# Half-wide one-hots by source-tile parity, and the input rows' inverse root made on GpSimd, in a graph network with a two-expert layer

## The chip, the cores and the metric

The kernel runs on one NeuronCore of a Trainium2 chip. Its engines work side by side, each from its own queue: TensorE (PE) multiplies, VectorE (DVE) and ScalarE (ACT) work elementwise, GpSimd (POOL) does a little, SyncE (SP) issues most DMAs. They hand work to each other through semaphores. The metric is the device time of one execution in microseconds (us); lower is better.

## The reference, cut to what matters

```python
deg  = segment_sum(ones, rows, N) + 1.0          # N = 6250 nodes, 100000 edges (rows, cols)
dinv = rsqrt(deg)[:, None]
h = layernorm(x) @ W_in + b_in                   # 256 features
for l in range(4):
    h_scaled = h * dinv
    msg = segment_sum(h_scaled[cols], rows, N) * dinv
    ctx = mean(h, axis=0) @ Wg[l] + bg[l]
    z = relu((h + msg) @ Wl[l] + bl[l] + ctx)
    h = layernorm(z) * gamma[l] + beta[l]
x = x + h
# then: x + layernorm(x + the two best of eight experts' feed-forward of layernorm(x))
```

`rows` is the input `src` and `cols` the input `dst`. The edges come sorted by `dst`.

## The kernel before

The kernel turns the edge list into a dense matrix of edge counts, the adjacency, of 49 by 49 tiles of 128 by 128 nodes in one byte each. It writes it to HBM and then, in each of the four layers, reads it back and multiplies the node table with it. The matrix is made in the first 512 us; the layers run until about 2830 us and the experts until the end.

The 100,000 edges lie in 782 blocks of 128, one per column, with an edge on each partition. For each destination tile `m` of 128 nodes the kernel takes a window of `WIN` = 18 neighbouring blocks. The destination one-hot `hot_d` says which of the tile's 128 nodes an edge goes to. The source one-hot `hot_s` is 540 wide: it has 11 columns (`LANES`) for each of the 49 source tiles, and twelve lanes share one column, told apart by the power of two in `src_w`, two bits each. The matmul of the two, summed over the window, gives for the tile's 128 nodes the counts of all sources, packed in words of 24 bits.

Four engines work on tile `m` or its neighbours at the same time:

- VectorE (`hots`, L713) makes the source one-hots, one per block (`tensor_scalar`, L724): 35 for each pair of tiles, since neighbouring windows overlap. Between them it makes the input rows' statistics (L731, L734), `mask` of the previous tile (L757, four shifts and masks over the words), `relative` (L700, the labels of the next window, whose start it loads into a register first, L699), the reciprocal and the bias of the row normalisation (L744, L747), and the label one-hots of the next tile (`hot_rows`, L708).
- TensorE (`counts`, L1269) multiplies, two matmuls of 270 columns for each block, and between them runs the transpose (`turn`, L1297) and the input product (`product`, L1302 and L1304) of the previous tile's normalised rows. Behind the counts come `degrees` of the previous tile (L1266, 49 matmuls of one column over the staged bytes) and `add_mean` (L1310).
- ScalarE (`extract`, L1102) takes the square root (L1105), copies the transpose out (xnT, L1108), runs `unpack` of the previous tile (L1094: twelve activations, each turning one two-bit field of the words into 11 lanes of bytes), normalises the next rows (xnb, L1112), copies the product (h0, L1100) and then the words of this tile (L1118).
- SyncE writes four tiles of staged bytes at a time to HBM (`write`, L493), from two halves of a buffer in turn.

The order on each engine is written out by hand and unrolled. `wait_ge` holds an engine until a semaphore has a value; nothing behind it on that engine starts earlier. The index of a one-hot's column, and the window's start, come from registers, which the engine's sequencer sets: these are the rows `ISA` and `TENSOR_LOAD` in the lists of order below.

Behind the last tile follow its degrees and product, a flag that says whether all edges were counted, the scales, and the first table copies on ScalarE (L1170), which overwrite the staging buffer and so wait for the last write.

## Time and profile before

| | |
|---|---|
| three runs | 3206.35, 3206.64 (median), 3207.5 us |
| the profiled execution | 3210.56 us, its span from first to last instruction 3208.6 us |
| TensorE's mean granted clock | 0.975 of full speed |
| busy over the span | PE 3076.7 us, DVE 1901.3, ACT 855.9, POOL 70.3 |
| from the words of tile 1 to those of tile 48 | 455.29 us, 49.12 to 504.41 |

The profile is of one execution. A row of a timeline has the start, the length, the engine, the line, the operation with what it writes and reads, and how many of them it groups; brackets give the idle time before it and what ended it. Operations of one engine overlap: the next starts before the one before has left the pipeline, so what one costs its engine is the distance of the starts, not its length. The clock column is the share of TensorE's full speed that was granted; 1.00 is 2.4 GHz and 0.50 is 1.2 GHz.

### The profile page before, as it was taken

To read this page: it belongs to the slowest core of one execution; us is meant where nothing else is said; L and a number is where in the kernel's file an instruction comes from. 1 tells how busy PE (TensorE), PEld (TensorE's weight loads), DVE (VectorE), ACT (ScalarE), POOL (GpSimd) and SP (SyncE) were. 2 spreads that over 40 slices of the span, in tenths; PEclk is the share of its full clock that TensorE was granted. 3 is DMA by queue.
4 is the path that set the end of the run, shared out by engine and by line. 5 is a ranking of instruction groups with operands and counts; after the bars stand their busy time and mean duration, and the time that the engine had idled before them with its cause. 6 is when DMAs were issued, how large, how long until landed. Compare 5 with 4: busy or idle time off the path is not lost.

```text
span 3208.6 us, 54202 instructions
## 1 busy us (share of the span) xinstructions
PE 3076.7 (96%) x17323; PEld 1804.0 (56%) x17323; DVE 1901.3 (59%) x5185; ACT 855.9 (27%) x1934; POOL 70.3 (2%) x168
## 2 busy tenths in 40 slices
PE   6999996999999999999999999999999999979998
PEld 4777773444444444444444444444444444468887
DVE  8999997555555545555554555555566666645554
ACT  4989896111111111111111111111111111132332
POOL 0000000000000000000000000000000000001010
PEclk9989996999999999999999999999999999989999
DMA  4323324122222222222222222222222222110000
GB/s 130 96 83 94 91 82 122 61 70 70 70 70 70 70 70 70 70 70 70 70 70 70 70 70 70 70 70 70 80 82 82 82 82 82 48 40 16 18 18 18
DMA packets 134110, 225.11 MB, mean 70 GB/s; under 512 B 12277, under 2 KB 106596, under 8 KB 134018
## 3 DMA queue, kind: packets, MB, share of 16 engines
q1 hardware_dynamic: 131666, 217.53, 20.9%
q0 software_dynamic: 2352, 6.40, 0.8%
q8 instruction: 52, 0.85, 0.1%
q14 instruction: 40, 0.33, 0.0%
HBM read 178.17 MB, written 45.74 MB: 70 GB/s over the span
## 4 chain that ended last, share of the span: by engine, by line
PE 84%; ACT 9%; DVE 3%; issue 2%; DMA 1%; SPq 0%; DVEq 0%; ACTq 0%; POOLq 0%; POOL 0%
PE bank L1416 64%; ACT tab L1094 7%; PE bank L1490 5%; PE bank L1496 5%; PE bank L1374 4%; PE bank L1364 1%; PE bank L1266 1%; PE bank L1286 1%; DVE later L757 1%; DMA tab<-in_x 1%; DVE region L724 1%; PE bank L1310 1%; ACT later L1118 0%; PE bank L1304 0%; ACT xnb L1112 0%
## 5 line engine op out<-in xcount | busy, mean ns | idle before, releaser
L1416 PE MATMUL bank<-tab,region 128*128 128x512 f16 x9604 | 2143.2, 380 | 14.3 <-DVE tab L840 14.0
L1416 PEld LDWEIGHTS bank<-tab,region 128*128 128x128 fp8e4 x9604 | 940.8, 98 | 1065.5 <-DVE tab L840 17.9
L1094 ACT ACTIVATE tab<-later 128x539 fp8e4<-128x539 uint8 x588 | 336.1, 674 | 1.9 <-DVE later L757 1.9
L724 DVE TENSOR_SCALAR region<-iota_w,src_col,src_w 128x540 bf16<-128x540 int16 x858 | 310.8, 415 | 0.4 <-issue 0.3
L941 DVE SCALAR_TENSOR_TENSOR region<-bank,c_back,later 128x256 f32<-128x256 f32 x196 | 94.8, 484 | 351.2 <-PE bank L1374 351.2
L1197 ACT ACTIVATE sd<-mv,eps_c 128x1 f32<-128x1 f32 x196 | 57.8, 295 | 817.6 <-DVE mv L948 817.6
L936 DVE TENSOR_TENSOR region<-bank,region 128x256 f16<-128x256 f32 x196 | 83.3, 425 | 287.7 <-ACT region L1193 287.7
L1193 ACT ACTIVATE region<-bank 128x256 f16<-128x256 f32 x196 | 75.3, 384 | 568.2 <-PE bank L1364 568.2
L1490 PE MATMUL bank<-tab 128*128 128x384 f32 (+1 forms) x544 | 178.0, 487 | 3.8 <-DMA b_s<-in_L_ffn_b 3.8
L1496 PE MATMUL bank<-tab 128*128 128x256 f32 (+1 forms) x784 | 175.5, 384 | 0.9 <-ACT tab L1221 0.9
L1490 PEld LDWEIGHTS bank<-tab 128*128 128x128 f32 x544 | 164.4, 310 | 13.4 <-issue 6.3
L1374 PE MATMUL bank<-later,region 128*128 128x256 f16 x1176 | 161.0, 273 | 0.9 <-DVE region L936 0.9
L1496 PEld LDWEIGHTS bank<-tab 128*128 128x128 f32 (+1 forms) x784 | 148.8, 192 | 22.3 <-ACT tab L1221 1.4
L1191 ACT ACTIVATE region<-bank 128x256 f32<-128x256 f32 x196 | 75.3, 384 | 294.0 <-PE bank L1416 294.0
L1161 ACT ACTIVATE tab<-region,c_write 128x256 f32 x147 | 74.6, 508 | 274.1 <-DVE region L957 274.1
L1374 PEld LDWEIGHTS bank<-later,region 128*128 128x128 f16 x1176 | 115.2, 98 | 56.3 <-DVE region L936 1.2
L1221 ACT ACTIVATE tab<-bank,b_s 128x384 f32<-128x384 f32 (+1 forms) x136 | 77.2, 568 | 249.3 <-PE bank L1490 249.3
L1286 PE MATMUL bank<-region 128*128 128x270 bf16 x900 | 131.0, 299 | 1.3 <-DVE region L708 0.8
L1286 PE MATMUL bank<-region,later 128*128 x864 | 129.3, 309 | 1.4 <-DVE region L724 1.4
L925 DVE TENSOR_TENSOR region<-bank,region 128x256 f32<-128x256 f32 x196 | 83.0, 423 | 73.9 <-ACT region L1191 73.9
L1286 PEld LDWEIGHTS bank<-region,later 128*128 128x128 f16 x864 | 112.7, 145 | 15.4 <-issue 2.5
L1286 PEld LDWEIGHTS bank<-region 128*128 128x128 f16 x900 | 108.7, 146 | 19.9 <-DVE region L724 1.8
(199 smaller groups left out, 2232.8 us busy)
## 6 DMA issues: line engine op xcount, KB each, us to landing
region<-adjacency SPq DMA_DIRECT2D x196, 784.0 KB, 4.3
adjacency<-tab SPq DMA_DIRECT2D x12, 3136.0 KB, 13.7
region<-in_x POOLq DMA_DIRECT2D x48, 128.0 KB, 2.3
out<-region SPq DMA_DIRECT2D x48, 128.0 KB, 1.7
tab<-in_x SPq DMA_DIRECT2D x1, 6016.0 KB
tab<-in_L_ffn_W SPq DMA_DIRECT2D x4, 512.0 KB, 4.7
region<-in_L_gnn_Wl SPq DMA_DIRECT2D x1, 1024.0 KB, 5.4
later<-in_L_gnn_Wg SPq DMA_DIRECT2D x1, 1024.0 KB, 9.4
```

What stands on the lines that cost most here:

```text
L724: v.tensor_scalar(hot_s[:, j, :], iota_w[:, 0:WP], src_col[:, ds(first_block[0] + j, 1)], src_w[:, ds(first_block[0] + j, 1)], ALU.is_equa ...
L925: tile_own.done(v.tensor_tensor(acc_s, acc[a][:, 0:D], lo_f[:, a, :], ALU.add))
L936: v.tensor_tensor(uT[:, 1, :, :], T3[3], uT[:, 0, :, :], ALU.subtract).then_inc(uT_split, 1)
L941: tile_own.done(v.scalar_tensor_tensor(out=Z, in0=bank[4][:, 0:D], scalar=c_back[:, ds(n, 1)], in1=bias[:], op0=ALU.mult, op1=ALU.add))
L1094: ins = a.activation(stage[h][:, :, slot, f * LANES:f * LANES + n], counts[:, :, 0:n], ACT.Copy, saturate=False)
L1191: a.activation(lo_f[:, s, :], acc[s][:, D:2 * D], ACT.Copy).then_inc(lo_ready, 1)
L1221: a.activation(gT[:, f, 0:w], bank[f % 3][:, 0:w], ACT.Gelu, bias=b1_s[:, f // FC, f % FC:f % FC + 1]).then_inc(gelu_done, 1)
L1286: ins = mm(bank[k % 2 * 2 + half][:, 0:HALFP], hot_d[m % 2][:, :, j], hot_s[:, block + j, half * HALFP:(half + 1) * HALFP], start=j == 0, ...
L1374: ins = mm(bank[4][:, 0:D], uT[:, a, k, :], Wx[:, b, l, k, :], start=q == 0, stop=q == len(parts) - 1)
L1416: ins = mm(acc[a][:, :], A_s[:, a, m, :], tab[:, here + m, :], start=m == 0, stop=m == T - 1)
L1490: ins = mm(bank[f % 3][:, 0:w], W1_s[:, f // FC * KC + k, f % FC:FF:FC], xfT[:, k, 0:w], start=k == 0, stop=k == KC - 1)
L1496: ins = mm(bank[5 + u][0:r, 0:D], gT[:, f, u * P:u * P + r], W2_s[:, f // FC, f % FC, :], start=f == 0, stop=f == TOP * FC - 1)
```

## The change

Each edge gets twice its destination plus the parity of its source tile as its label, and windows go by half tiles: 64 destinations times two parities are again 128 labels. A destination tile has two half windows of `HALF_WIN` = 10 blocks. Partition `2 d + odd` of a result then holds destination `d` of the half and source tiles of one parity only, so `hot_s` needs 11 columns for each of 25 source tiles: 275, made 276 wide. Four half windows, that is two tiles, share one run of 35 source one-hots.

- TensorE runs 20 matmuls of 275 columns per tile where it ran 36 of 270. Its step registers are loaded three times per pair of tiles (once before). `degrees` has 50 matmuls of two columns, and runs for tile `m - 2` behind the counts of tile `m`, where it ran for `m - 1`.
- ScalarE's `unpack` has five activations over three (or two) fields at a time, in two pairs of shifts with h0 between them. xnT and the next tile's xnb come ahead of the unpack. The square root is gone from this stage.
- VectorE makes the statistics two tiles ahead, no longer makes reciprocal and bias, does the mask behind the fourth one-hot, and `relative` loads two starts. Its setup has four more passes over all blocks. The statistics of tile 2, in tile 0, now wait for all input rows.
- GpSimd makes the inverse root by a power and the bias, for two tiles at a time, in four operations.
- SyncE writes each group of four tiles by four DMAs, by half and parity.
- Buffers move: the words and masks no longer lie in `later`.

```diff
+HALF_WIN = 10
+WIN = 2 * HALF_WIN
+GROUP = 4
+STEP = HP * NE // (N * P)
+SLOTS = (GROUP - 1) * STEP + STEP_HI + HALF_WIN
...
+                for odd in range(2):
+                    n = TI - odd
+                    for e in range(2):
+                        sp.dma_start(A[odd::2, e * HP:(e + 1) * HP, ds(m0, width), :].rearrange("t p m s -> p t (m s)"),
+                                     stage32[h][odd::2, e * TI:e * TI + n, 0:width * P // 4]).then_inc(a_written[h], 16)
...
+            for g in range(TI):
...
+                root_own.done(nc.gpsimd.tensor_tensor(xrs[:, g % 2, 0:n], xsd[:, 0:n], halves2[:, 0:n], ALU.pow))
+                root_own.wait()
+                nc.gpsimd.tensor_tensor(xnb_bias[:, g % 2, 0:n], xneg[:, 0:n], xrs[:, g % 2, 0:n],
+                                        ALU.mult).then_inc(xscale_ready, 1)
...
+                if m > 1:
+                    dve.wait_ge(hot_d_ready, m - 1)
+                for e in range(2):
+                    start = dve.value_load(starts[0:1, 2 * m + e:2 * m + e + 1], min_val=0, max_val=COLS - HALF_WIN)
+                    ins = v.tensor_scalar(drel[m % 2][:, e * HALF_WIN:(e + 1) * HALF_WIN], dstf[:, ds(start, HALF_WIN)],
+                                          tile_base[:, 2 * m + e:2 * m + e + 1], None, ALU.subtract)
...
+                for at, j in enumerate(range(split, SLOTS) if second else range(split)):
...
-                    if k and at == 6:
+                    if k and at == 3:
                         mask(m - 1, (k - 1) % 2)
+                    if m + 2 < T and at == (5 if m else 10):
+                        spread(m + 2)
+                    if m + 2 < T and at == (6 if m else 11):
+                        moments(m + 2)
...
+                act.wait_ge(xnT_done, m + 1)
+                a.activation(xnT[:], T3[4], ACT.Copy).then_inc(xnT_copied, 1)
+                if m + 1 < T:
+                    normal(m + 1)
+                unpack(m, (0, 1))
+                h0(m)
+                unpack(m, (2, 3))
...
+                        mm(bank[k % 2 * 2 + e][:, 0:WP], hot_d[m % 2][:, :, e * HALF_WIN + j], hot_s[:, block + j, 0:WP],
+                           start=j == 0, stop=j == HALF_WIN - 1).then_inc(hot_used, 1)
+                if m > 1:
+                    degrees(m - 2)
                 if k:
-                    degrees(m - 1, k - 1)
                     add_mean(m - 1, mean_w)
```

VectorE, from the mask of one tile to the first one-hot behind the labels, before (L757 mask, L724 one-hot, L699 and L700 the labels):

```order
L757 TENSOR_SCALAR later<-later 128x1080 [waits staged,words_ready]
L757 TENSOR_SCALAR later<-later 128x1080 x3
L724 ISA [waits hot_used]
L724 TENSOR_SCALAR region<-iota_w,src_col,src_w 128x540
...
L699 TENSOR_LOAD starts
L699 ISA x2
L700 ISA
L700 TENSOR_SCALAR drel<-dstf,tile_base 128x18
```

The same engine after, from the statistics of the tile after next to the labels (L779 one-hot, L760 and L765 statistics and aggregate, L740 and L741 the labels):

```order
L760 BN_STATS xst<-tab 128x6 [waits xscale_ready,xvar_ready,x_in]
L779 ISA [waits hot_used]
L779 TENSOR_SCALAR region<-iota_w,src_col,src_w 128x276
L765 BN_AGGR xmv<-xst 128x2 [waits xst_ready]
...
L740 TENSOR_LOAD starts [waits hot_d_ready]
L740 ISA x2
L741 ISA
L741 TENSOR_SCALAR drel<-dstf,tile_base 128x10
L740 TENSOR_LOAD starts
L740 ISA x2
L741 ISA
L741 TENSOR_SCALAR drel<-dstf,tile_base 128x10
```

Statistics and aggregate now stand between the mask and the labels, three one-hots ahead of them, and the register load with its operation is there twice.

TensorE behind the counts, before and then after. The names are the same; L1266 is L1327 now, L1310 is L1374, L1275 is L1340 and L1297 is L1361:

```order
L1266 MATMUL bank<-one_b,tab 128x1 [waits staged]
L1266 MATMUL bank<-one_b,tab 128x1 x48
L1310 MATMUL bank<-tab,mean_w 128x256 [waits h0_ready]
L1275 TENSOR_LOAD steps [waits words_ready]
L1275 ISA x2
L1297 MATMUL bank<-ident,xnb 128x128 [waits xn_ready]
```

```order
L1327 MATMUL bank<-odd_b,tab 128x2 [waits staged]
L1327 MATMUL bank<-odd_b,tab 128x2 x49
L1374 MATMUL bank<-tab,mean_w 128x256 [waits h0_ready]
L1340 TENSOR_LOAD steps [waits words_ready]
L1340 ISA x2
L1361 MATMUL bank<-ident,xnb 128x128 [waits xn_ready]
```

The rows stand as they stood, but `staged` is now asked for the tile before last, and `h0_ready` comes ahead of the unpack's second half.

ScalarE through one tile, before and after (L1094 and L1151 with L1155 unpack, L1118 and L1173 words, L1108 and L1176 xnT, L1112 and L1166 xnb, L1100 and L1162 h0):

```order
L1118 ACTIVATE later<-bank 128x270 x2
L1105 ACTIVATE xsd<-xmv,eps_c 128x1
L1108 ACTIVATE xnT<-bank 128x256
L1094 ACTIVATE tab<-later 128x49x11 x11
L1094 ACTIVATE tab<-later 128x49x7
L1112 ACTIVATE xnb<-tab,xnb_bias,xrs 128x256
L1100 ACTIVATE tab<-bank 128x256
```

```order
L1173 ACTIVATE region<-bank 128x275 x2
L1176 ACTIVATE xnT<-bank 128x256
L1166 ACTIVATE xnb<-tab,xnb_bias,xrs 128x256
L1151 ACTIVATE tab<-region 128x50x3x11 x2
L1162 ACTIVATE tab<-bank 128x256
L1151 ACTIVATE tab<-region 128x50x3x11
L1151 ACTIVATE tab<-region 128x50x2x11
L1155 ACTIVATE tab<-region 128x50x7
```

xnb and h0 stood behind the unpack, directly ahead of the words; now the unpack's second half ends the tile.

## Rows read from the trace of the kernel before

**Rows 1.** Busy time in a stretch: length, PE, PEld, DVE, ACT, POOL, clock, DMA, GB/s.

```profile
49.12:504.41 455.29, 418.51 (x4476) 345.14 (x4473) 433.12 (x1285) 406.49 (x848) 0.00 (x0) 0.93 0.28 80
```

**Rows 2.** Groups by line and shape in that stretch, ScalarE: busy, mean ns, idle.

```profile
L1094 ACT ACTIVATE tab<-later 128x539 fp8e4<-128x539 uint8 x517 | 303.6, 690 | 0.0
...
L1105 ACT ACTIVATE xsd<-xmv,eps_c 128x1 f32<-128x1 f32 x47 | 13.9, 295 | 0.0
```

**Rows 3.** Timeline of ScalarE over one tile.

```profile
302.21 0.67 ACT L1118 ACTIVATE later<-bank 128x270 int32<-128x270 f32 x2
...
303.86 0.39 ACT L1108 ACTIVATE xnT<-bank 128x256 f32<-128x256 f32 x1 [0.79 <-PE bank L1297]
304.14 6.85 ACT L1094 ACTIVATE tab<-later 128x539 fp8e4<-128x539 uint8 x12
310.89 0.58 ACT L1112 ACTIVATE xnb<-tab,xnb_bias,xrs 128x256 f32<-128x256 f32 x1
...
311.65 0.66 ACT L1118 ACTIVATE later<-bank 128x270 int32<-128x270 f32 x2
```

**Rows 4.** Timeline of TensorE, from the degrees to the transpose.

```profile
301.70 1.36 PE L1266 MATMUL bank<-one_b,tab 128*128 128x1 bf16 x49
...
303.44 0.38 PE L1297 MATMUL bank<-ident,xnb 128*128 128x128 f32 x2
```

**Rows 5.** Busy time in stretches of 2 us, columns as in rows 1.

```profile
348.00:350.00 2.00, 0.99 (x14) 0.64 (x14) 1.99 (x7) 2.00 (x5) 0.00 (x0) 1.00 0.00 0
352.00:354.00 2.00, 2.00 (x11) 1.47 (x10) 2.00 (x8) 1.70 (x4) 0.00 (x0) 0.50 1.02 286
```

**Rows 6.** Timeline of ScalarE in narrow windows within the unpack; neighbouring pairs overlap.

```profile
306.35 1.29 ACT L1094 ACTIVATE tab<-later 128x539 fp8e4<-128x539 uint8 x2
...
307.01 1.38 ACT L1094 ACTIVATE tab<-later 128x539 fp8e4<-128x539 uint8 x2
...
307.54 1.33 ACT L1094 ACTIVATE tab<-later 128x539 fp8e4<-128x539 uint8 x2
```

**Rows 7.** Timeline of VectorE in the same tile: mask, label rows, one-hots.

```profile
302.92 1.49 DVE L757 TENSOR_SCALAR later<-later 128x1080 uint16<-128x1080 uint16 x4 [0.59 <-ACT later L1118]
...
306.63 1.35 DVE L708 TENSOR_TENSOR later<-rep,drel 128x2304 f16<-128x2304 f16 x1
307.90 2.41 DVE L724 TENSOR_SCALAR region<-iota_w,src_col,src_w 128x540 bf16<-128x540 int16 x7
```

**Rows 8.** Groups by line and shape, 49.12 to 504.41 us, VectorE, as rows 2.

```profile
L724 DVE TENSOR_SCALAR region<-iota_w,src_col,src_w 128x540 bf16<-128x540 int16 x819 | 296.7, 415 | 0.2
L757 DVE TENSOR_SCALAR later<-later 128x1080 uint16<-128x1080 uint16 x188 | 70.1, 437 | 18.4 <-ACT later L1118 18.1
...
L731 DVE BATCH_NORM_STATS2 xst<-tab 128x6 f32<-128x256 f32 x46 | 19.4, 421 | 0.0
L700 DVE TENSOR_SCALAR drel<-dstf,tile_base 128x18 f16 x46 | 10.8, 235 | 0.0
```

**Rows 9.** Timeline at the start; line L699, register loads: ns min/median/max, first and last start.

```profile
26.41 0.24 DVE L700 TENSOR_SCALAR drel<-dstf,tile_base 128x18 f16 x1 [1.72 <-issue]
...
L699 DVEq TENSOR_LOAD <-starts x49: 301/313/946, 25.7 to 485.9; - x49
```

**Rows 10.** Timeline of VectorE in tile 1.

```profile
38.94 0.43 DVE L731 BATCH_NORM_STATS2 xst<-tab 128x6 f32<-128x256 f32 x1 [2.02 <-DMA tab<-in_x]
```

**Rows 11.** Timeline behind the last tile: the product, the first table copies.

```profile
515.22 2.08 PE L1304 MATMUL bank<-Win_s,xnT 128*128 128x256 f32 x4
...
523.45 19.65 ACT L1170 ACTIVATE tab<-tab,c_write  x49 [1.47 <-DVEq L826]
```

**Rows 12.** DMA issues: queue, count, KB each, median us from issue to landing.

```profile
adjacency<-tab SPq DMA_DIRECT2D x12, 3136.0 KB, 13.7
...
adjacency<-tab SPq DMA_DIRECT2D x1, 784.0 KB, 8.7
```

**Rows 13.** Groups by line and shape over the span, GpSimd.

```profile
L612 POOL TENSOR_TENSOR rs<-sd,half_c 128x1 f32<-128x1 f32 x48 | 26.4, 550 | 8.8 <-POOL sd L610 4.2
```

More of the change, by code:

```diff
@@ L104, in build @@
 def build(nc, x, src, dst, W_in, b_in, Wl, bl, Wg, bg, gamma, beta, Wr, br, W1, b1, W2, b2, fgamma, fbeta, out):
-    assert all(e * DIV >> 11 == e // LANES for e in range(P)) and 2 * PARTS <= 24 and 2 * PAIRS == T - 1
+    assert all(e * DIV >> 11 == e // LANES for e in range(P)) and 2 * PARTS <= 24 and PARTS == 12 and T % 2
+    assert GROUP * GROUPS == 4 * TI and COLS >= NB + SLOTS - HALF_WIN and COLS <= CH * P
     assert RING * LOOP == T - 1 and 2 * MG * MLOOP == T - 1 and NB <= 2 * 512 and FIELDS <= 10
@@ L276, in build @@
         sd2 = sb("sd2", [P, 1])
+        hsum = sb("hsum", [P, D])
+        bias = sb("bias", [P, D])
         Wr_s = sb("Wr_s", [P, KC, EX])
@@ L1079, in _, with unpack @@
                 act.sem_inc(s, 1)
[L1082 removed]
+            def unpack(m, shifts):
+                k = (m - 1) % (2 * MG) + 1 if m else 0
+                i = (m - 1) // (2 * MG) if m else 0
                 h, slot = k // MG % 2, k % MG
[L1084 to L1086 removed]
+                if shifts[0] == 0 and slot == 0:
+                    act.wait_ge(a_written[h], AW * (i + k // (2 * MG) + 1))
                     act.wait_ge(deg_done, m + 1)
[L1089 to L1096 removed]
+                for f in shifts:
+                    at = slot * P + f * LANES
+                    last = f == 3
+                    lift = 3 * LANES if slot == MG - 1 and not last else 0
+                    bytes_in = PARTS // 4 - last
+                    hold(act, masks_ready, m * 4 + f + 1)
+                    lanes = stage[h][:, :, at - lift:at - lift + bytes_in * 4 * LANES].rearrange("p q (b z) -> p q b z", b=bytes_in)
+                    ins = a.activation(lanes[:, :, :, lift:lift + LANES], masked8[:, f, :, 0:bytes_in, :], ACT.Copy,
+                                       saturate=False)
+                    if last:
+                        n = P - 11 * LANES
+                        ins = a.activation(stage[h][:, :, at + 8 * LANES:at + 8 * LANES + n], masked8[:, f, :, 2, 0:n],
+                                           ACT.Copy, saturate=False)
+                if last:
+                    ins.then_inc(staged, 1)
             def h0(t):
@@ L1253, in _ @@
                     pe.wait_ge(before_set, 1)
-                    mm(bank[4][0:1, 0:T], ones[:, 0:1], before[:], start=True, stop=True).then_inc(starts_sum, 1)
+                    mm(bank[4][0:1, 0:GROUP * GROUPS], ones[:, 0:1], before[:], start=True, stop=True).then_inc(starts_sum, 1)
             pe.wait_ge(hot_ready, 1)
@@ L1260, in clear, with degrees @@
                 return mm(bank[6][:, 0:FIELDS * PK], zero_b[:], zero_b[:, 0:FIELDS * PK], start=start, stop=not start)
-            def degrees(m, k):
+            def degrees(m):
+                k = (m - 1) % (2 * MG) + 1 if m else 0
                 h, slot = k // MG % 2, k % MG
                 hold(pe, staged, m + 2)
-                for t in range(T):
-                    ins = mm(bank[6][:, t:t + 1], stage[h][:, t, slot, :], one_b[:], start=False, stop=False)
+                for q in range(2 * TI):
+                    i = q % TI
+                    ins = mm(bank[6][:, 2 * i:2 * i + 2], stage[h][:, q, slot * P:(slot + 1) * P], odd_b[:], start=False,
+                             stop=False)
                 ins.then_inc(deg_done, 1)
@@ L1321, in _ @@
             ins.then_inc(norms_done, 1)
-            degrees(T - 1, 2 * MG)
             product(T - 1)
+            degrees(T - 2)
+            degrees(T - 1)
             add_mean(T - 1, mean_last).then_inc(h0_summed, 1)
```

303 lines of the change are left out of this document (153 added, 150 removed).

## The prediction, made before the change was run

> **What bounds the kernel now.** I read the busy time by stage first [rows 1]. The stage that the diff touches runs from about 27 us to 512 us. From the second tile's words to the last tile's it takes 455.29 us for 47 tiles, 9.69 us a tile (517 wide unpacks are 47 tiles of 11 [rows 2]), and in it TensorE is busy 418.51 us, VectorE 433.12 and ScalarE 406.49. No engine has slack, so a cheaper engine alone buys little: the order of hand-overs decides.
>
> One undisturbed tile shows them. ScalarE copies the words at 302.21 and again at 311.65: 9.44 us apart [rows 3]. Between lie the wait for TensorE's transpose, xnT, 12 unpacks in 6.75 us (304.14 to 310.89) and xnb with h0 (0.76). The words end 0.67 after their start, at 302.88, but xnT starts only at 303.86, because TensorE came to the transpose at 303.44: it ran the degrees (from 301.70, when the unpack had ended) and the mean before it [rows 4]. So the cycle is unpack, degrees, mean, transpose, xnT, unpack. The difference between 9.44 and the mean of 9.69 is time in which TensorE's granted clock was lower: it stood at 0.50 (the 1.2 GHz level) at 352 to 354 us, behind a stretch in which TensorE was busy 0.99 of 2 us and then ran the one-column degrees [rows 5].
>
> **ScalarE's part.** Per tile 6,272 elements in 12 instructions become 6,400 in 5; the square root (295 ns) goes, the words stay two of nearly the same width. At the present mean rate that is 6.9 us. Neighbouring starts are 0.53 us apart at best (307.01, 307.54 [rows 6]) for 539 elements: by that rate 6.3. Between a one-element activation (295 ns) and a 539-element one (690 ns) [rows 2] lie 0.73 ns an element, which leaves 0.17 us of the mean interval of 0.56 as fixed: 5 fixed parts and 6,400 elements give 5.5. I take 6.1, just under the best observed rate, as fewer fixed parts must count for something; ends 5.5 and 6.9. From the transpose's start to the next words' end ScalarE takes 312.31 - 303.44 = 8.87 now, so 8.87 - 6.75 + 6.1 = **8.2 us** after.
>
> **TensorE's part.** The 36 matmuls of 270 columns become 20 of 275, some 2 us less; they were never last. What matters is the order: the degrees are now those of two tiles back, so they and the mean no longer wait for the unpack but run right behind the counts. That takes the 0.98 us gap between words and xnT to about 0.5 wherever TensorE arrives first. If it comes later, the counts' end sets the transpose: from the degrees' start to the transpose 1.74 us (301.70 to 303.44), with the last matmul and its semaphore about 1.95 us. The odd tile's register load of its step, ahead of the transpose, waits for the words as now; there are two more such loads in the middle of the counts, which the product covers.
>
> **VectorE's part.** 35 one-hots per two tiles remain 35 (19 in the even tile, 16 in the odd), only narrower. The 540-wide ones start 0.33 us apart (7 in 2.41 us [rows 7], 415 ns each); the mask, twice as wide, takes 437 ns [rows 8] and starts every 0.35 us (four in 1.49). Twice the width for about the same time says that most of a one-hot is fixed: 0.26 ns an element from the mask's rate, so 264 fewer elements save 0.07 and the one-hot takes **0.26 us**, not half of 0.33. Its ends are the 0.14 us of the 18-wide operation (235 ns, its last 0.1 overlapped [rows 8]) and the present 0.33. The label rows go 2,304 to 2,560 wide: 1.27 us (306.63 to 307.90) becomes 1.40. The mask is unchanged at 1.43. The reciprocal and the bias go to GpSimd (0.2 us off).
>
> What is added: the row of relative labels now loads two registers instead of one, and it stands only three one-hots behind the aggregate that waits for the statistics, so the sequencer has no lead. What a load costs without a lead shows at the start: VectorE stood 1.72 us idle for two [rows 9]. Less the three one-hots' 0.79, with the two small operations, that is 1.2 us from the ninth one-hot to the next. Now one load per tile costs nothing, since mask and three one-hots are queued ahead of it.
>
> An even tile, from the words: mask 0.06 + 1.43, fourteen one-hots to the last one's start 3.7, statistics (421 ns, 0.34 of it exposed) and aggregate 0.5, labels 1.2, label rows 1.4, the last one-hot's own 0.35: 8.6 us. With TensorE's 1.95 the transpose can start at **10.5**. ScalarE alone would be back with the next words at 8.2, so here it waits. An odd tile has three one-hots fewer (9.7).
>
> **Sum of the stage.** ScalarE's next words follow that transpose by 8.2: two tiles take 10.5 + 8.2 = 18.7, or 9.37 each. The odd tile's chain hides in this: VectorE, which can take the next mask at 9.5, ends that tile's chain at 9.5 + 9.7 = 19.2, 0.5 behind the even tile's words, and ScalarE's 8.2 + 0.5 still arrives before 9.5. So the bound moves from ScalarE with TensorE to VectorE, TensorE, ScalarE in turn. For the lower clock I keep the present 0.25 us a tile: 9.62 against 9.69, over 47 tiles **-3 us**.
>
> **Before and after it.** VectorE waited for the input rows until 38.94 in tile 1 [rows 10]; that wait now stands at the eleventh one-hot of tile 0, as the statistics are made two tiles ahead. Behind it come the label rows, the rest of tile 0's one-hots, the words and one unpack: words of tile 1 end near 52.7 instead of 49.8, **+3 us**. It also covers the longer setup of VectorE (some 4 us of integer passes; 2 to 3 us of cover are left, and without it they count in full). At the end h0 stands between the last tile's unpacks and needs the product, which ends near 517.3 now (515.22 + 2.08 [rows 11]) at the lower clock, behind the norms. In the new order that is about 7.7 us after the last words; with the rest of the unpack the tile is staged at 11 rather than 7.5. The last write, 8.7 us to landing [rows 12], holds ScalarE's table, which starts 18.4 us after the words now (523.45) and near 21 then: **+2.5 us**. The flag is not later, since the product no longer follows the degrees.
>
> GpSimd's part: ScalarE's xnb now waits for its bias instead of VectorE's. The statistics are ready some 2.7 us after the words of one tile and used some 10 us after them, in the next; four operations at 0.55 us at most [rows 13] are 2.2 us, and if each had to stand behind a 1.35 us label row, 7.6. So it is hidden, with no margin only in that worst case. The writes become four of a quarter each: 13.7 us to landing now [rows 12], against the 37 us that four tiles give. Nothing behind the stage changes.
>
> Total: -3 + 3 + 2.5 = +2.5 us on the profiled 3208.6 (3210.56 with what lies around it); on the median of 3206.64 that is **3209 us**.
>
> **Rivals.**
> *ScalarE's instructions were mostly overhead.* With 5.5 us for the unpack two tiles take 18.1, about VectorE's own floor (9.5 + 8.7): 9.1 a tile, 9.35 with the clock, -16 + 5.5: **3196 us**. For it: the starts of equal activations differ (0.66 from 306.35 to 307.01, then 0.53), so something other than elements counts. Against: 0.53 us for 539 elements is already near one a nanosecond. The Trainium skill, VectorE: DVE Perf Modes, on the SBUF-source errata, has 224 cycles fixed per ScalarE instruction at 1.2 GHz; as a saving of seven of these per tile that would be 1.3 us and an unpack of 5.5.
> *The register loads take over (slower).* The present loads last 301 to 946 ns [rows 9], median 313. At 0.6 each the even tile gets 0.6 longer, 9.67 a tile, 9.92 with the clock: +11 + 5.5, **3223 us**; at 0.94 each 3238. It decides from about 0.5 us a load. For it: they stand back to back. Against: the median. The Trainium skill, DMA: Bandwidth & Descriptors, latency facts, gives 600 ns as the floor of a tensor load; the median here is below.
> *TensorE's clock falls oftener (slower).* It has 3 us less work in the same period and longer gaps: behind the counts come 1.25 us of degrees, and VectorE's label rows open 1.4 us in the counts. If the loss doubles to 0.5 us a tile: +9 + 5.5, **3221 us**. Against: a lower clock hits only the mean, the transpose and matmuls that VectorE paces anyway.
> *The narrow one-hot is no cheaper* (0.33 us): 1 us more per even tile, 3234 us; at 0.14 ScalarE with TensorE would bound at some 8.6 us a tile, near 3173. The rows make both unlikely; they belong to the tails.
>
> **Chances.** Forecast case 0.38 (3203 to 3215, almost all of it within 0.2%, that is within 6.4 us, about what a measurement of this kernel can tell from no change; 0.03 of it above). ScalarE gains more: 0.28. Loads 0.17, clock 0.15, the one-hot no cheaper 0.02. So faster by over 0.2%: 0.28; within 0.2%: 0.35; slower: 0.37. The range, 3190 to 3226, leaves about 0.08 below and 0.1 above.
>
> **What the changed profile would show.** One-hots near 350 ns, starting 0.26 apart (near 0.19: half-priced after all); an idle gap on VectorE before the label operations, near 0.8 us (over 1.5: loads); the five unpacks in 6.1 us less h0; alternating distances of words, short then long, 18.7 per pair; the transpose right behind the mean in odd tiles, behind the words in even ones; tile 1's words near 52; the last write's landing and the first table copy about 21 us behind the last words. Equal distances near 8.9, VectorE waiting at the mask in every tile, would mean that the chain I name is not there. A granted clock under 0.9 over the stage would speak for the third rival.

## The result, and the profile after

| | changed | before |
|---|---|---|
| median (range) | 3241.76 us (3240.85 to 3244.63) | 3206.49 us (3206.09 to 3207.5) |
| ratio, 95% interval | 1.0111 (1.0094 to 1.0129) | |
| profiled span | 3243.0 | 3208.6 |
| to the words of tile 1 | 54.16 | 49.12 |
| tile 1 to tile 48 | 487.50, 10.37 a tile | 455.29, 9.69 a tile |
| last words to the end of the span | 2701.3 | 2704.2 |

The change makes the kernel 1.1% slower, outside the range given. Of the 34.4 us between the spans the 47 tiles hold 32.2, the start 5.0, and what follows gives 2.9 back.

The whole stretch, as [rows 1] of before (length, PE, PEld, DVE, ACT, POOL, clock, DMA, GB/s):

```profile
54.16:541.66 487.50, 423.85 (x3764) 299.14 (x3762) 393.39 (x1238) 385.79 (x471) 30.31 (x92) 0.75 0.26 74
```

VectorE has 40 us less to do than before and ScalarE 21, in a longer time. TensorE has 16% fewer matmuls and is busy longer: its granted clock is 0.75, where it was 0.93. Two neighbouring tiles show both levels. ScalarE, as [rows 3]:

```profile
314.43 0.68 ACT L1173 ACTIVATE region<-bank 128x275 int32<-128x275 f32 x2
315.60 0.39 ACT L1176 ACTIVATE xnT<-bank 128x256 f32<-128x256 f32 x1 [0.50 <-PE bank L1361]
315.88 0.59 ACT L1166 ACTIVATE xnb<-tab,xnb_bias,xrs 128x256 f32<-128x256 f32 x1
316.37 3.28 ACT L1151 ACTIVATE tab<-region 128x1650 fp8e4<-128x1650 uint8 x2
319.55 0.36 ACT L1162 ACTIVATE tab<-bank 128x256 f32<-128x256 f32 x1
319.80 2.94 ACT L1151 ACTIVATE tab<-region 128x1650 fp8e4<-128x1650 uint8 x2
322.63 0.50 ACT L1155 ACTIVATE tab<-region 128x350 fp8e4<-128x350 uint8 x1
323.41 0.69 ACT L1173 ACTIVATE region<-bank 128x275 int32<-128x275 f32 x2 [0.28 <-PE bank L1351]
326.18 0.38 ACT L1176 ACTIVATE xnT<-bank 128x256 f32<-128x256 f32 x1 [2.08 <-PE bank L1361]
326.46 0.59 ACT L1166 ACTIVATE xnb<-tab,xnb_bias,xrs 128x256 f32<-128x256 f32 x1
326.96 3.27 ACT L1151 ACTIVATE tab<-region 128x1650 fp8e4<-128x1650 uint8 x2
331.24 0.38 ACT L1162 ACTIVATE tab<-bank 128x256 f32<-128x256 f32 x1 [1.01 <-PE bank L1368]
331.52 2.96 ACT L1151 ACTIVATE tab<-region 128x1650 fp8e4<-128x1650 uint8 x2
334.36 0.51 ACT L1155 ACTIVATE tab<-region 128x350 fp8e4<-128x350 uint8 x1
334.75 0.69 ACT L1173 ACTIVATE region<-bank 128x275 int32<-128x275 f32 x2
```

The first tile takes 8.98 us, less than any of before (9.42 at the least). The second takes 11.34: xnT waits 2.08 us for the transpose, and h0 (L1162), now in the middle of the unpack, 1.01 us for the product. TensorE from the end of the first tile on, and the clock (column before last but two):

```profile
322.49 0.89 PE L1351 MATMUL bank<-region 128*128 x3 [1.33 <-DVE region L779]
323.21 1.44 PE L1327 MATMUL bank<-odd_b,tab 128*128 128x2 bf16 x50
324.52 1.20 PE L1374 MATMUL bank<-tab,mean_w 128*128 128x256 f32 x2
325.51 0.63 PE L1361 MATMUL bank<-ident,xnb 128*128 128x128 f32 x2
325.94 2.05 PE L1351 MATMUL bank<-region 128*128 128x275 bf16 x8
327.92 1.22 PE L1366 MATMUL bank<-bin_s,ones 1*128 1x256 f32 x2
329.06 2.08 PE L1368 MATMUL bank<-Win_s,xnT 128*128 128x256 f32 x4
```
```profile
320.00:322.00 2.00, 0.91 (x4) 0.43 (x3) 2.00 (x5) 2.00 (x2) 0.00 (x0) 1.00 0.02 4
322.00:324.00 2.00, 1.51 (x34) 1.26 (x35) 1.91 (x8) 1.72 (x4) 0.00 (x0) 0.94 0.03 8
324.00:326.00 2.00, 2.00 (x30) 1.67 (x28) 1.86 (x6) 0.10 (x1) 0.00 (x0) 0.50 0.00 0
328.00:330.00 2.00, 2.00 (x4) 1.25 (x5) 1.48 (x6) 2.00 (x2) 0.00 (x0) 0.50 0.00 0
```

Behind the 1.33 us in which VectorE made the label rows and the 1.4 us of two-column degrees the clock goes to 0.50, the 1.2 GHz level, and stays there until about 333. Mean, transpose, counts and product all lie in that stretch. At full clock the mean takes 0.68 us, bias row and product 0.69 and 1.13.

Where engines waited in the 47 tiles (us, times, longest):

```profile
ACT xnT L1176 <- PE bank L1361: 55.3, 39, 2.1
DVE drel L741 <- issue: 49.3, 90, 1.2
ACT tab L1162 <- PE bank L1368: 33.3, 25, 2.6
```

The first stood at 46.2 us before. The second (register loads) and the third (h0 for the product) are new: before, the label operation never waited [rows 8]. TensorE's own register loads, which the change makes three in two tiles, show no such wait: its counts stood idle 63.7 us in these tiles, 62.5 of them for one-hots.

### The profile page after: what moved, and what is told of

Read it like the earlier page. It is cut to its first block, busy times and chain, and to the rows that moved or that the text cites. A ratio compares the mean times of both kernels' runs of the same rounds, so it can differ in the third digit from the quotient of the medians.

```text
span 3243.0 us, 52744 instructions
## 1 busy us (share of the span) xinstructions
PE 3072.5 (95%) x16588; PEld 1750.8 (54%) x16588; DVE 1862.0 (57%) x5142; ACT 835.5 (26%) x1543; POOL 103.0 (3%) x270
## 4 chain that ended last, share of the span: by engine, by line
PE 90%; DVE 3%; ACT 2%; issue 2%; DVEq 1%; DMA 1%; SPq 1%; ACTq 0%; POOLq 0%; POOL 0%
PE bank L1481 63%; PE bank L1555 5%; PE bank L1561 5%; PE bank L1351 5%; PE bank L1439 4%; PE bank L1368 2%; PE bank L1327 2%; PE bank L1429 1%; PE bank L1366 1%; PE bank L1374 1%; DVE region L779 1%; ACT tab L1151 1%; DMA tab<-in_x 1%; DVE region L803 1%; DVEq L773 0%
## 5 line engine op out<-in xcount | busy, mean ns | idle before, releaser
L1151 ACT ACTIVATE tab<-region 128x1650 fp8e4<-128x1650 uint8 x196 | 304.9, 1615 | 0.4 <-DVE region L803 0.4
L1351 PE MATMUL bank<-region 128*128 (+1 forms) x980 | 230.0, 373 | 74.4 <-DVE region L779 71.3
L994 DVE SCALAR_TENSOR_TENSOR region<-bank,c_back,bias 128x256 f32<-128x256 f32 x196 | 94.8, 484 | 350.9 <-PE bank L1439 350.9
L779 DVE TENSOR_SCALAR region<-iota_w,src_col,src_w 128x276 bf16<-128x276 int16 x859 | 245.8, 346 | 0.8 <-issue 0.5
L1351 PEld LDWEIGHTS bank<-region 128*128 128x128 f16 x980 | 147.3, 155 | 154.3 <-issue 87.5
L1439 PE MATMUL bank<-Wx,region 128*128 128x256 f16 x1176 | 160.5, 273 | 0.9 <-DVE region L989 0.9
L1439 PEld LDWEIGHTS bank<-Wx,region 128*128 128x128 f16 x1176 | 115.0, 98 | 56.1 <-DVE region L989 1.2
L893 DVE SCALAR_TENSOR_TENSOR tab<-region,c_write,tab 128x256 f32 x147 | 71.2, 485 | 73.0 <-ACT tab L1220 73.0
L982 DVE SCALAR_TENSOR_TENSOR region<-region,c_own 128x256 f32<-128x256 f32 x196 | 95.0, 485 | 24.2
```

The costliest lines, as they stand in the source:

```text
L779: v.tensor_scalar(hot_s[:, j, :], iota_w[:, 0:WS], src_col[:, ds(first_block[0] + j, 1)], src_w[:, ds(first_block[0] + j, 1)], ALU.is_equa ...
L982: v.scalar_tensor_tensor(out=U[:, 0, :], in0=hs, scalar=c_own[:, ds(t, 1)], in1=Q, op0=ALU.mult, op1=ALU.add).then_inc(u_ready, 1)
L994: tile_own.done(v.scalar_tensor_tensor(out=Z, in0=bank[4][:, 0:D], scalar=c_back[:, ds(n, 1)], in1=bias[:], op0=ALU.mult, op1=ALU.add))
L1151: ins = a.activation(lanes[:, :, :, lift:lift + LANES], masked8[:, f, :, 0:bytes_in, :], ACT.Copy, saturate=False)
L1351: mm(bank[k % 2 * 2 + e][:, 0:WP], hot_d[m % 2][:, :, e * HALF_WIN + j], hot_s[:, block + j, 0:WP], start=j == 0, stop=j == HALF_WIN - 1). ...
L1439: ins = mm(bank[4][:, 0:D], uT[:, a, k, :], Wx[:, b, l, k, :], start=q == 0, stop=q == len(parts) - 1)
```

## Experiments

Times are medians; ratios are to runs of the kernel before on the same chip, whose median lay between 3206.5 and 3208.6 us, so small differences between rows that were not measured side by side (the groups are e1 to e4, e5 to e8, e9 to e12, e13 to e16, e17 and e18) are safer read from the ratios. Gains over the changed kernel are given below as differences of medians; by the ratios they are 2 to 4 us larger, and those of e5, e6 and e8 have intervals that overlap the changed kernel's. "Clock" and "us a tile" are those of the stage in the profiled run, tile 1 to 48.

| run | base and edit | clock | us a tile | median us | ratio (95%) |
|---|---|---|---|---|---|
| changed | | 0.75 | 10.37 | 3241.76 | 1.0111 (1.0094 to 1.0129) |
| e1 | changed, counts doubled | 0.92 | 10.18 | 3233.13 | 1.0072 (1.0055 to 1.0089) |
| e2 | changed, label gap filled | 0.93 | 10.04 | 3227.12 | 1.0057 (1.0039 to 1.0074) |
| e3 | changed, h0 last | 0.78 | 10.06 | 3228.48 | 1.0059 (1.0043 to 1.0076) |
| e5 | changed, loads behind the mask | 0.78 | 10.22 | 3234.72 | 1.0081 (1.0064 to 1.0098) |
| e6 | changed, transpose early | 0.76 | 10.24 | 3237.87 | 1.0091 (1.0075 to 1.0108) |
| e7 | changed, adjacency written twice | 0.73 | 10.75 | 3276.23 | 1.0211 (1.0194 to 1.0228) |
| e8 | e5 and e6 | 0.75 | 10.34 | 3238.56 | 1.0093 (1.0077 to 1.0110) |
| e9 | changed, loads apart | 0.81 | 9.74 | 3213.14 | 1.0014 (1.0004 to 1.0024) |
| e10 | e9, h0 last, TensorE's loads | 0.74 | 9.79 | 3213.79 | 1.0017 (1.0005 to 1.0028) |
| e11 | e10, transpose early | 0.80 | 9.09 | 3182.10 | 0.9928 (0.9910 to 0.9946) |
| e12 | e11, label gap filled | 0.89 | 9.37 | 3193.77 | 0.9958 (0.9943 to 0.9973) |
| e14 | e11, label rows in halves | 0.81 | 9.00 | 3179.60 | 0.9914 (0.9897 to 0.9932) |
| e15 | e11, degrees spread | 0.79 | 9.67 | 3206.24 | 0.9996 (0.9986 to 1.0005) |
| e16 | e14 and e15 | 0.83 | 9.53 | 3204.02 | 0.9991 (0.9981 to 1.0002) |
| e18 | e14, last six counts doubled | 0.89 | 9.21 | 3189.06 | 0.9933 (0.9917 to 0.9950) |
| e4 | before, degrees two tiles back | 0.98 | 9.20 | 3185.20 | 0.9932 (0.9916 to 0.9949) |
| e13 | e4, half the columns left out | 0.82 | 9.36 | 3192.96 | 0.9953 (0.9937 to 0.9969) |
| e17 | e4, root and bias on GpSimd | 0.99 | 9.04 | 3176.07 | 0.9902 (0.9885 to 0.9918) |

**Is it the columns?** Three runs change how much TensorE multiplies. e1 and e2 add matmuls of no use; e13 leaves out matmuls, and with them half of the edge counts, so it does not compute the adjacency. Beyond that e13 changes only the comparison behind the flag, so that the rest runs the same way.

```diff
 # e1, ahead of each count matmul
+mm(bank[5][:, 0:D], hot_d[m % 2][:, :, e * HALF_WIN + j], hot_s[:, block + j, 0:D], start=False, stop=False)
 # e2, ahead of one count of a tile
+if (e, j) == ((1, 7) if m % 2 else (1, 4)):
+    for _ in range(10):
+        mm(bank[5][:, 0:D], zero_b[:], rep[:, 0:16, 0:16], start=False, stop=False)
 # e13, on e4
-for half in range(2):
+for half in range(2 if j in (0, WIN - 1) else 1):
```

> The changed kernel; ahead of each of the 20 count matmuls of a tile stands a second one of the same operands (256 columns) into an unused half of a PSUM bank. Theory A (the 20 narrow count matmuls leave TensorE with too few columns, so its granted clock falls): the stage's granted clock returns from 0.74 to over 0.9, the distance of words from 10.37 us to 9.0 to 9.4, and the time to 3185 to 3200. Rival B (the new order is slow in itself, the low clock goes beside it): 20 more matmuls can only add, 3242 or more. Rival C (both: clock up, but the added 2.2 us of matmul work stand in the chain): 9.6 to 9.9 us a tile, 3205 to 3225.

> The changed kernel with ten matmuls of 256 columns and no use, in one place only: where TensorE waits while VectorE makes the label rows (before the fifth count matmul of the second half in even tiles, the eighth in odd). Theory A1 (this gap with the degrees behind it is what lowers the clock): granted clock over 0.9, 3185 to 3205. A2 (the columns missing over the whole tile lower it; 2560 of the 4220 missing come back): clock between, 0.8 to 0.9, 3205 to 3230. Rival B (the order is slow in itself): clock may rise, time stays at 3235 to 3245 or more.

> e4 (the kernel before with the degrees of two tiles back), in which 16 of the 18 count matmuls of the words' second half are left out, so that half of the adjacency counts is missing; the order, VectorE's work and every wait stay. Theory A (columns): the granted clock of the stage falls from 0.98 to under 0.85, and the time does not fall below e4's 3185. Theory A1 (gap and degrees, not the columns): the clock stays over 0.93 and the time within 5 us of e4.

e4 and e13, tile 1 to tile 48:

```profile
49.78:482.08 432.30, 418.27 (x4465) 341.57 (x4465) 429.16 (x1285) 409.14 (x848) 0.00 (x0) 0.98 0.30 84
```
```profile
50.35:490.43 440.08, 398.48 (x3713) 283.80 (x3713) 431.60 (x1285) 405.86 (x847) 0.00 (x0) 0.82 0.29 82
```

VectorE and ScalarE do the same in both, and no wait was added; 752 matmuls are gone, and the clock goes from 0.98 to 0.82. So leaving out matmuls, and nothing else, lowered it: this is shown, and theory A1 (gap and degrees without the columns) fell. But the loss is small, 0.17 us a tile, 7.8 us in all (net of whatever the missing matmuls themselves saved): in that order little waits for TensorE. In e1 and e2, in the changed order, the clock came back to 0.92 and 0.93, as theory A had it, but only 9 and 15 us of the 35 came with it (0.4 and 0.5% by the ratios). That is short of theory A and against B, which had no gain at all; no theory had both the clock and the time. In e2 31 tiles ran at 0.95 or more of full clock, and their mean was still 9.84 us. So the clock costs the changed kernel about 10.37 - 9.84 = 0.5 us a tile (an estimate, as the fillers take time of their own), and something else about as much again.

**Which waits turn it into time?** e3 moves h0, e6 the transpose.

```diff
 # e3
-unpack(m, (0, 1))
+unpack(m, (0, 1, 2, 3))
 h0(m)
-unpack(m, (2, 3))
 # e6
-if k and e * HALF_WIN + j == TURN_AT:
-    turn(m - 1)
-if k and e * HALF_WIN + j == PRODUCT_AT:
-    product(m - 1)
+if e * HALF_WIN + j == PRODUCT_AT:
+    if k:
+        product(m - 1)
+    turn(m)
```

> The changed kernel with ScalarE's h0 behind the whole unpack (as before) and not in its middle. Its wait for the product was 27.5 us between 100 and 500 us. If this wait is a cost of its own (theory D): 20 to 30 us less, 3212 to 3222, at an unchanged low clock. If the clock sets the tile and the wait is one of its forms (theory A): the late product is hidden, 10 to 25 us less, but distances of words still between 8.9 and 10.5, and the clock stays under 0.8. If VectorE, TensorE and the transpose set it anyway (rival E): under 5 us less.

> The changed kernel with the transpose of tile m made behind the product of tile m-1, in the middle of tile m's counts (its input xnb is ready by then), instead of behind counts, degrees and mean. ScalarE's wait for it (43.7 us between 100 and 500 us) goes. Theory A (the low clock costs by stretching degrees, mean, transpose and product): the granted clock stays under 0.8, but costs less, 9.8 to 9.9 us a tile, 3215 to 3222. Theory G (VectorE's loop sets even tiles): the same 9.8 and not less, since VectorE's loop does not contain the transpose. If ScalarE with TensorE set every tile, 9.0 to 9.3 and 3180 to 3192.

e3 gains 13 us at a clock of 0.78, within theory A's range and short of theory D's: the place of h0 costs that much at nearly the same clock. It is less than the 33.3 us of its wait, since another wait grew, that for the transpose, from 55.3 us:

```profile
ACT xnT L1176 <- PE bank L1360: 76.2, 47, 2.2
```

e6 removed the wait for the transpose and gained 4 us, which is hardly clear of noise and slower than all three forecasts. Between 100 and 500 us h0's wait went from 27.5 to 61.9 us:

```profile
ACT tab L1162 <- PE bank L1368: 61.9, 40, 2.9
```

**The register loads.** e5, e7 and e9 try them.

```diff
 # e5: both loads behind the mask; e9: load(m + 1, 1) there,
 # and load(m + 2, 0) behind the label rows of tile m + 1
 mask(m - 1, (k - 1) % 2)
+loaded[m + 1] = load(m + 1)
 # e7
-for odd in range(2):
+for B, odd in ((A, 0), (A, 1), (A2, 0), (A2, 1)):
```

> The changed kernel with the two register loads of the next label row right behind the mask, where VectorE still has 1.4 us of mask work queued, instead of straight ahead of the operations that use them. In the changed kernel VectorE stood 41.6 us idle between 100 and 500 us at those operations (0.75 us a tile, 2.2 in the tile that meets an adjacency write). Theory G (words, mask, loads, one-hots, counts, words is a loop that sets even tiles): the idle goes, even tiles get 0.8 to 1.1 us shorter, odd ones little: 3205 to 3222. Theory A (the clock alone sets it): under 8 us less. If both loops were equal everywhere, 40 us less, 3200.

> The changed kernel with each adjacency write sent twice, the second time to another tensor that nothing reads. Theory W (a register load that meets the write takes about 1 us instead of 0.3, and these stand in VectorE's loop): the write lasts some 21 of 40 us instead of 11, two of four tiles have the slow loads, VectorE's idle there goes from 41.6 to 55 to 60 us between 100 and 500 us, and the time rises by 8 to 15 us, to 3250 to 3257. If the write has no part in it: within 3 us of 3242.

> The changed kernel with VectorE's two register loads of a label row apart: one behind the label rows of the tile before (1.5 us of queued work), one behind the mask (1.4 us). In e5 both stood behind the mask, and in the tile that meets the adjacency write they outlasted it (VectorE idle 1.36 us, TensorE 2.76, then clock 0.50, the product 3.3 us, h0 late by 4.07, 12.3 us for the tile), while undisturbed tiles fell to 8.6. Theory W (loads that meet the write open the gap in TensorE's work, and clock, product and h0 follow): the 12.3 us tiles go to 9.5 to 10.5, the mean from 10.2 to 9.5 to 9.8, 3200 to 3215. Theory A (the columns alone lower the clock, with or without the gap): mean 10.0 or more, 3225 or more.

That a load gets slow beside an adjacency write shows in e2, where the clock does not blur it. The loads of two tiles without a write, those of the next tile (ns min/median/max), and that stretch with its DMA share (last but one):

```profile
L740 DVEq TENSOR_LOAD <-starts x4: 298/302/314, 270.2 to 280.8; - x4
```
```profile
L740 DVEq TENSOR_LOAD <-starts x2: 952/1015/1078, 289.8 to 291.2; - x2
```
```profile
288.00:292.00 4.00, 3.90 (x21) 2.74 (x19) 2.51 (x10) 3.93 (x4) 1.31 (x4) 1.00 1.01 285
```

VectorE then stood idle for 0.87 and 1.30 us ahead of the two label operations; without a write it was 0.23 or 0.42 ahead of the first and 0.52 ahead of the second. e7 agrees: with the write sent twice that idle time rose from 41.6 to 55.0 us (100 to 500 us), as expected. The stage grew by 17.7 us, somewhat more than expected; 13.4 us more come behind it, where the last write's landing is waited for, which the forecast had left out.

e5 gained 7 us, which is the figure of theory A, but not for its reason. In some undisturbed tiles the distance fell to 8.5 or 8.6 us, but every fourth, the one that meets the end of a write, took 12.1 on average. One of these, on VectorE, on TensorE and on ScalarE:

```profile
259.95 1.52 DVE L812 TENSOR_SCALAR region<-region 128x1100 uint16<-128x1100 uint16 x4 [1.37 <-ACT region L1182]
262.82 0.61 DVE L786 TENSOR_SCALAR region<-iota_w,src_col,src_w 128x276 bf16<-128x276 int16 x2 [1.36 <-issue]
```
```profile
263.23 0.60 PE L1360 MATMUL bank<-region 128*128 128x275 bf16 x2 [2.76 <-DVE region L786]
264.08 0.81 PE L1360 MATMUL bank<-region 128*128 128x275 bf16 x2 [0.25 <-DVE region L786]
264.82 1.22 PE L1375 MATMUL bank<-bin_s,ones 1*128 1x256 f32 x2
265.97 2.08 PE L1377 MATMUL bank<-Win_s,xnT 128*128 128x256 f32 x4
```
```profile
268.14 0.39 ACT L1171 ACTIVATE tab<-bank 128x256 f32<-128x256 f32 x1 [4.07 <-PE bank L1377]
```

The two slow loads outlast the mask by 1.36 us, TensorE starves for 2.76, its clock is then 0.50 (264 to 270 us), the product is slow, and h0 comes 4.07 us late into the unpack. e9 puts one load behind the label rows and one behind the mask. It gains 29 us against the changed kernel, within its forecast, and e5's tiles of 12 us are down to 10.7 on average (11.3 at most), a little over the 9.5 to 10.5 that was expected. No other single edit of the changed kernel gave as much: the register loads, with the chain of waits behind them, were its dearest part. But e9 covers all loads and not only those that meet the write. By the place of a tile against the write (11 or 12 tiles each, us a tile) it went from 10.36 to 9.25 in the tile in which most of the write falls, from 10.65 to 10.69 in the next, and from 9.59 to 8.94 and from 10.89 to 10.04 in the two without a write. So about 12 of the 30 us in the stage came beside the write and 18 in tiles whose loads took 0.3 us.

**All loops at once.** e8 joins e5 and e6 and gains nothing over either, 40 us and more above both its forecasts: it still has the tiles of 12 us at the end of each write, as the slow loads still starve TensorE. From e9 on they have cover.

> Both edits of the two runs before it together: transpose early and register loads behind the mask. With neither VectorE's loads nor the transpose in a loop, ScalarE's own work (words 0.69, xnT and xnb 0.9, unpack and h0 6.8) and VectorE's loop without loads (9.0 even, 8.4 odd) remain: 8.7 to 9.0 us a tile and 3163 to 3180. If the low clock of TensorE still costs in counts and product: 9.1 to 9.4, 3182 to 3198.

> e9 with h0 behind the whole unpack and with TensorE's own register loads (three in two tiles, in front of counts) moved behind the transpose and behind the product, where its queue holds fp32 matmuls. Theory W with D: every load has cover and no late product stops the unpack: 9.0 to 9.3 us a tile and 3180 to 3195, the clock still low in part. Theory A: the clock at half speed still stretches counts, mean and transpose: 9.5 or more, 3205 or more.

> e10 with the transpose of tile m made behind the product in the middle of tile m's counts. Nothing on TensorE then stands between words and unpack but the counts themselves. ScalarE's work is 8.5 us, VectorE's loop 8.9 in even tiles and 8.2 in odd: 8.7 to 9.0 us a tile, 3168 to 3180. If low clock in the counts themselves (0.3 us a tile and more) is what is left: 9.1 to 9.4, 3182 to 3200.

e10 gained nothing over e9. It missed its first forecast and lies in that of theory A, with a wait that neither had named: h0 behind the unpack freed ScalarE, but TensorE's mean, which stands ahead of the transpose, now waited for h0 (19.2 us ahead of its weight load), and ScalarE waited for the transpose in all 47 tiles:

```profile
ACT xnT L1188 <- PE bank L1379: 55.1, 47, 2.1
PEld bank L1392 <- ACT tab L1174: 19.2, 21, 1.3
```

With the transpose in the middle of the counts (e11) both waits are off ScalarE's way, and the same move that gave 4 us in e6 gives 32 (by the ratios 6 and 29). At 3182 and 9.09 it ends at the near edge of its second forecast, that low clock in the counts is left. Whether moving TensorE's own loads in e10 had a part in it was not tried apart.

e11's tiles at full clock take 8.01 and 8.79 in turn, 8.40 on average, and its mean is 9.09: some 0.7 us a tile goes with the tiles of lower clock. Four runs tried to get it back.

```diff
 # e14: hot_rows in two operations
-if m < T - 1 and at == 12:
-    hot_rows(m + 1)
+if m < T - 1 and at == 12:
+    hot_rows(m + 1, 0, HP)
+if m < T - 1 and at == 14:
+    hot_rows(m + 1, HP, P)
 # e15: behind each count
+degrees(m - 2, range(2 * TI)[3 * (e * HALF_WIN + j - 1):3 * (e * HALF_WIN + j)])
 # e18, ahead of each count with e == 1 and j >= 4: the doubled matmul of e1
```

> e11 with the ten useless matmuls of 256 columns in the label rows' gap (as e2). If the low clock still costs in e11, this takes it back: clock over 0.9 and 5 to 20 us less than e11. If e11 has no loop left with TensorE in it: equal to e11 within 3 us. If the fillers stand in the way (1.1 us of work, 2.2 at half clock): slower than e11 by 5 us or more.

> e11 with the label rows in two operations of half the width (0.75 us each), two one-hots apart, so that TensorE's gap in the counts is two short ones. Theory A1 (the gap lowers the clock): fewer low tiles, clock from 0.79 to 0.9, 8.6 to 8.8 us a tile, 3160 to 3172. Theory A (columns over a tile): clock still 0.75 to 0.83 and 3178 to 3186.

> e11 with the 50 degree matmuls, three behind each of the counts from the second on, instead of all in a row of 1.4 us behind the counts. Their columns stay. If the long row of two-column matmuls lowers the clock: 0.79 to 0.9 and 8.6 to 8.8 us a tile, 3160 to 3172. If the columns of the tile alone do it: the clock stays, but 1.4 us of TensorE's tail is filled into its waits: 3170 to 3182. If they hinder the counts at half clock: 3185 to 3195.

> e14 with the last six of a tile's 20 count matmuls doubled (256 columns each, no use), ahead of the degrees. If columns in that stretch keep the clock: over 0.9, 8.5 to 8.7 us a tile and 3155 to 3168. If the tiles at half clock get longer by the doubled work (as in e12) as much as there are fewer of them: 3176 to 3190.

None did by more than noise. e12 and e18 raised the clock to 0.89, and 30 and 31 tiles ran at full clock where e11 had 19; but the tiles with the lowest clock (under 0.75) now took 11.5 and 11.2 us on average instead of 10.1, as the fillers run at half speed too: ten of them took up to 2.10 us where they take 1.25 at full clock. e14 came out as theory A had it, 0.81 and 3180, with times that overlap e11's: TensorE's gap at the label rows, 0.88 us in one piece in a tile of e11 (at 159 us) and at most 0.66 in one of e14 (at 161 us), did not keep the clock when it was split. e15 lost 24 us, more than its worst forecast: at full clock a count with three degrees takes 0.24 us (264.21 to 264.45), near the 0.26 at which VectorE makes one-hots, so TensorE can hardly catch up (the likely reason; no run shows it apart):

```profile
264.21 0.32 PE L1370 MATMUL bank<-region 128*128 x1
264.37 0.22 PE L1339 MATMUL bank<-odd_b,tab 128*128 128x2 bf16 x3
264.45 0.32 PE L1370 MATMUL bank<-region 128*128 x1
```

e16, both together, was forecast at 3150 to 3162 or 3170 to 3182 and took 3204, as e15 did: the halved label rows did not help there either.

**Parts of the change alone, on the kernel before.**

```diff
 # e4
-degrees(m - 1, k - 1)
+if m > 1:
+    degrees(m - 2, ...)
 ...
 # e17, on GpSimd, for one tile at a time; ScalarE's Sqrt and VectorE's reciprocal and bias go
+root_own.done(nc.gpsimd.tensor_tensor(xrs[:], xsd[:], half_c[:], ALU.pow))
+nc.gpsimd.tensor_tensor(xnb_bias[:], xneg[:], xrs[:], ALU.mult).then_inc(xscale_ready, 1)
```

> The kernel before with one part of the change alone: the degrees of two tiles back behind the counts, not those of one. Theory A (fewer columns lower the clock): the columns are those of before, so the clock stays at 0.9 or over and the time is 3190 to 3207, as the degrees no longer wait for the unpack. Rival F (the place of the degrees, straight behind counts that VectorE paces, lowers the clock): clock under 0.85 and 3215 or more.

> e4 (before, degrees of two tiles back) with the inverse root and the bias of the input rows made on GpSimd, one tile at a time; ScalarE's square root and VectorE's reciprocal and bias go. VectorE was busy 99.8% of e4's stage, so its 0.2 us a tile come off in full if GpSimd's four operations (about 2 us) are hidden: 3174 to 3180. If VectorE's or ScalarE's wait for GpSimd is late: 3185 or more. The clock stays at 0.97 to 0.98.

e17 came as forecast, e4 5 us below its forecast. ScalarE's wait for the transpose fell from 46.2 to 20.0 us in e4, and the degrees' new place did not lower the clock (0.98). e17 has the shortest time of all, 1% below the kernel before. So two parts of the change are worth 21 and 9 us (by the ratios 22 and 10; the intervals of e4 and e17 just touch), and the rest, the narrow one-hots with what they need (two loads per tile, longer label rows, fewer columns, the new order of ScalarE), takes 66 us on top of them: 3241.76 against 3176.07.

Most of these 66 us are the order of the work with its waits, not the narrow one-hots: e14, which keeps them and mends the waits, takes 3179.60, and its interval overlaps e17's. So at their best here the narrow one-hots gain nothing. In tiles at full clock they do: 8.34 us on average in e14's 19, 9.01 in e17's 45. The other 28 tiles of e14, at lower clock, give it back.

## Why the prediction was wrong

**Where it held.** A one-hot takes 346 ns and starts 0.26 us after its neighbour; the label rows 1.40 (320.59 to 321.99); GpSimd was hidden. Between the ninth one-hot and the next the undisturbed tile lost 1.2 us, with 0.23 and 0.52 us idle. The last words to the first table copy are 20.8 us (562.49), from the words' end, as the prediction counted, 20.1, foreseen near 21. At full clock many of e2's tiles took 9.76 us; the forecast's terms for an even tile (VectorE's 8.6, a last matmul of 0.34, the words' own 0.69) make 9.6. One reading behind the one-hot's price does not come out of its rows: the mask's 0.35 us for 1,080 elements is 0.32 ns an element at most, and 0.20 against the 18-wide operation's 0.14 us, not 0.26. With these the price would have been 0.24 to 0.28 us, so nothing hung on it.

**"For the lower clock I keep the present 0.25 us a tile."** This step failed. The third rival named the right cause and nearly the price (0.5 us a tile; the estimate from e2 is 0.53), but was given a chance of 0.15. Measured as in e2, by the mean of the tiles at 0.95 or more of full clock, the kernel before lost 9.69 - 9.51 = 0.18 us a tile, so the loss went up threefold where it was kept as it was. The argument against that rival, that a low clock hits only mean, transpose and paced matmuls, holds in e13, which has about the same loss of clock (0.16) and pays 0.17 us a tile. It is false of the changed kernel, since its ScalarE waits for mean and transpose, and the product too, through h0 in the unpack. That h0 needs the product was seen, but only for the last tile.

**The register loads.** The rival had 0.94 us a load for all tiles or a median of 0.31, and decided by the median. The maximum of [rows 9] was no stray value: it is the load beside a write, and one tile in four meets one. Idle time at the labels is 49.3 us over 46 tiles, 1.07 each, where some 0.8 was forecast: near 0.8 in three tiles of four, 2.1 in the fourth. With the waits behind all of them e9 shows 29 us. That the 3238 us of the case of 0.94 us a load lies near the measured 3241.76 is luck, as most loads took 0.3 us and the clock had its part.

**ScalarE's unpack.** 6.1 us was taken; 316.37 to 319.55, 319.80 to 322.63 and 334.36 to 334.75 make 6.40. Seven instructions fewer, at 128 elements more, saved 0.35 us, about 0.07 each. The first rival's 5.5 us did not come, and with it not the saving that the prediction worked out from the Trainium skill, VectorE: DVE Perf Modes (errata on the SBUF source), of 1.3 us.

**The start.** Forecast +3, it was +5.0: the wait for all input rows, moved as foreseen, ended at 40.60 and not at 38.94. Why they landed 1.7 us later no run shows:

```profile
40.60 0.43 DVE L760 BATCH_NORM_STATS2 xst<-tab 128x6 f32<-128x256 f32 x1 [5.46 <-DMA tab<-in_x]
```

**The end.** Forecast +2.5; the table copies start 1.8 us later behind the words (20.8 against 19.0), but VectorE's half of the tables, which stopped some 0.3 us before each group of seven, now runs through (42 in a row), and ends 42.2 us behind the last words where it took 42.9. From the last words to the end it is 2.9 us less; where the other 2.2 come from is open.

```profile
566.37 17.46 DVE L893 SCALAR_TENSOR_TENSOR tab<-tab,c_write  x42 [0.17 <-ACT tab L1229]
```

The sum then: 0.75 us a tile over the forecast's 9.62 is 35 us. Of it, as an estimate, about 0.3 is clock (0.53 against 0.25) and 0.3 loads (1.07 against 0.8); the rest, some 0.2, fits the longer unpack, which no run shows by itself. The wait of h0 in the middle of the unpack, which e3 prices at 13 us, lies across these shares. They are not independent either: e9 moved only loads, and the clock rose with it from 0.75 to 0.81. So two rivals, clock and loads, came true together; the prediction had priced each alone, and the range stopped short of their sum.

## What to carry to other kernels

Less work for an engine whose clock falls with it, as TensorE's did in e13, is not free: first list which of its instructions somebody waits for, at half speed, in the new order and not in the old. A maximum in a row is worth a look at when it occurs; if it comes with something periodic, it is a price per period. And where several loops are nearly as long, undoing one shows little (4 us for the transpose alone), and the same edit can show 32 us once the others are gone.

## What the runs showed of the hardware

- A register load from SBUF took about 0.3 us, and 0.95 to 1.08 us while the core's DMA engines were all busy with the adjacency write (share 1.01). It did so on both engines that load registers: TensorE's ranged from 295 to 993 ns in the changed kernel. The Trainium skill, DMA: Bandwidth & Descriptors (latency facts), has a floor of 600 ns; the trace has values on both sides of it.
- In e17, with VectorE busy 99% of the stage, GpSimd's power of one column lasted 597 ns to 2011, with a median of 1942; in the changed kernel, with VectorE at 81%, that of two columns took 702 on average. That VectorE's work is the cause is not shown. The four operations were still hidden.
